# Windowed attention layers: exponentials read from PSUM, with the negated maximum as bias

## The chip, the cores and the metric

One core of a Trainium2 chip runs the whole program. The metric is the device time of one execution in microseconds: 2783.15 us, the median of three runs of the kernel before (2777.86 to 2783.55).

## The reference

The program is a chain of four blocks on a tensor of 4 sequences x 512 tokens x 128 channels. The last block, which the change touches, is six layers of windowed attention with a gated feed-forward part. One layer, for one sequence, cut to what matters:

```python
qkv = shift_tokens(x) @ Wqkv                   # 128 -> 3 x 16 heads x 64
q, k = l2norm(q) * qs, l2norm(k) * ksc         # per head
q = q * cos * scale + rotate_half(q) * sin * scale
k = k * cos / scale + rotate_half(k) * sin / scale
sim = einsum('bhwie,bhwje->bhwij', bq, bk2) * 8.0   # windows of 32, own and previous
sim = where(mask, -big, sim)
x = softmax(sim) @ v, all heads, @ Wo + x
xn = layernorm(shift_tokens(x)) * g + b
x = (a * gelu(gate)) @ W2 + b2 + x             # a, gate = xn @ W1 + b1
```

## The kernel before

The function `windowed_layers` works in 24 rounds (6 layers x 4 sequences, `ROUNDS`). A round is one sequence through one layer: four tiles of 128 tokens, and for the scores eight blocks of 64 query tokens. Each engine runs its own fixed list of steps (`ORDER`), written out by hand once per turn, and the same list is repeated turn after turn; the number of dashes behind a step says how many rounds it lags behind the turn. So three or four rounds are in flight together, and the engines are held together only by semaphores. An engine does its list strictly in order: a step that waits holds everything behind it.

The steps of one round, in the order of the data:

- SyncE `xdK` loads tile K of the input into `xs`. TensorE `PK.J` (four per tile) and `VK.J` (two per tile) are the projections, 128x512 each, into the two banks `psP`; projection u waits until the bank of projection u-2 has been read.
- ScalarE `SqK.J` squares a projection; VectorE `RK.J` sums the squares per head; VectorE `ABK.J` makes the two products of the rotation; GpSimd `ad` adds them; VectorE `Ra` makes the norms of two tiles; GpSimd `nm` multiplies by them. ScalarE `Ve` copies the values.
- TensorE `TK.J` transposes into the one bank `psT`, ScalarE `Te` copies it out to `qT` or `kT`.
- TensorE `SK.0` computes the scores of block K for all 16 heads: first the mask with a bf16 matmul (line 1544), then 32 recorded small matmuls (line 1550) into the two banks `psS[0]` and `psS[1]`, 4 groups of 96 key columns in each. VectorE `XaK.J` (twice per block) takes the maximum of each 96 columns (line 1673), waits for it, and subtracts it while moving the scores to `pb` in SBUF (line 1674). ScalarE `XeK.0` takes exp(8 x) of all 128x768 in place (line 1616). VectorE `XdK.0` sums and takes the reciprocal (lines 1680, 1681), GpSimd `XnK.0` multiplies (line 1738).
- TensorE `AtK.J` transposes the probabilities into the one bank `psA`, ScalarE `PtK.J` copies it out, TensorE `AvK.J` multiplies with the values, ScalarE `OtK.0` copies to `oT`.
- The tail of a round uses the one bank `psF`: TensorE `wo0` and `wo1` (output projection, eight recorded 128x512 matmuls each, line 1479), VectorE `xf` (line 1685) adds to `H`, SyncE `xfd` loads the shifted copy, TensorE `tr` transposes it (line 1486), VectorE `ln` normalises (lines 79, 81, 62 to 71, 85), TensorE `back` transposes back (line 1490), ScalarE `xn` scales, then three times: TensorE `gN` (gate), ScalarE `ggN` (gelu, line 1637), TensorE `aN`, VectorE `hN` (line 1695); at last TensorE `w2` (line 1504) and VectorE `out` (line 1699).
- SyncE `tl` loads the weights of the tail once per layer (`load_tail`, lines 1434 to 1439) after the last `out` of the layer before; `wo0` waits for it.

Two waits that matter below, in the kernel before: `S` waits for the subtractions of the block before (semaphore `x1`), since these free the banks `psS`; and ScalarE needs a table load each time it goes from gelu to exp or back (there are two changes each way in a turn of the list before: `Xe4`, `gg0`, `Xe5`, `Xe6`, `gg1`, `gg2`, `Xe7`).

## Time and profile before

| quantity | value |
|---|---|
| median of three runs | 2783.15 us |
| profiled execution | 2780.95 us, span 2779.2 us |
| TensorE matmul busy | 2521.7 us (91%) |
| VectorE busy | 2322.9 us (84%) |
| ScalarE busy | 1624.5 us (58%) |
| GpSimd busy | 1483.7 us (53%) |
| granted TensorE clock, mean | 0.948 |
| span of the six layers | about 995 to 2773 us |

The windowed layers take about 1778 of the 2779 us. The busy shares over the span mix stages with different limits, so the share inside this stage is what counts. On the timelines an instruction's record is longer than its place in the queue where instructions overlap: the distance from one start to the next is its pace, and the sum of paces against the length of a turn tells how much an engine waits.

### The profile page before, as it was taken

The numbers are of one execution on the slowest core, as the hardware profiler recorded it, in microseconds if no ns is written. First come the engines' busy times: TensorE is split into PE (matmuls) and PEld (weight loads), VectorE is DVE, ScalarE is ACT, GpSimd is POOL, SyncE is SP. The second block draws the span as 40 slices with busy tenths as digits, with TensorE's granted clock in tenths as the row PEclk, the third lists the DMA queues.
The fourth block names the chain that finished last, engine by engine and source line by source line (L and its number), as shares of the span: only waits on it lengthen the run. The fifth ranks groups of instructions, "written<-read, shape, count | busy, mean of one in ns | idle before, by whom it ended". The sixth has DMA issues, their size and how long they took to land. (4 is left out here: it accounts for less than half of the span.)

```text
span 2779.2 us, 60743 instructions
## 1 busy us (share of the span) xinstructions
PE 2521.7 (91%) x21942; PEld 1632.1 (59%) x21942; DVE 2322.9 (84%) x4920; ACT 1624.5 (58%) x2742; POOL 1483.7 (53%) x1226
## 2 busy tenths in 40 slices
PE   7589866999997758999999999999999999999996
PEld 4267634777774425666666666666666656666662
DVE  5878744777775678999999999999999989999982
ACT  2123224888884235666666666666666656666662
POOL 2500002767771056666666666666666656666650
PEclk9799977999997789999999999999999999999997
DMA  1000001000000021111111111111111111111110
GB/s 55 1 7 6 7 3 39 24 23 23 23 16 1 1 90 26 30 30 53 25 51 30 53 25 45 30 50 28 45 30 53 30 43 29 27 29 45 35 26 19
DMA packets 45487, 83.65 MB, mean 30 GB/s; under 512 B 13365, under 2 KB 27173, under 8 KB 44072
## 3 DMA queue, kind: packets, MB, share of 16 engines
q1 hardware_dynamic: 45224, 80.12, 10.7%
q8 instruction: 168, 2.75, 0.4%
q14 instruction: 95, 0.78, 0.1%
...
## 5 line engine op out<-in xcount | busy, mean ns | idle before, releaser
L1528 PE MATMUL w_psP<-w_qkv,w_xs 128*128 128x512 f32 x1152 | 607.3, 610 | 42.0 <-DVE w_bb L1653 28.3
L1728 POOL TENSOR_TENSOR w_ab<-w_ab,w_bb 128x512 f32<-128x512 f32 x384 | 486.0, 1274 | 173.1 <-DVE w_bb L1653 172.9
L1733 POOL TENSOR_TENSOR w_ab<-w_ab,w_nrm 128x512 f32<-128x512 f32 x384 | 395.6, 1044 | 112.4 <-DVE w_nrm L67 112.4
L1738 POOL TENSOR_TENSOR w_pb<-w_pb,w_sm 128x768 f32<-128x768 f32 x192 | 282.3, 1470 | 303.4 <-DVE w_sm L1681 303.4
L1593 ACT ACTIVATE w_sq<-w_psP 128x512 f32<-128x512 f32 x384 | 229.3, 597 | 226.3 <-PE w_psP L1528 157.9
L1012 POOL TENSOR_TENSOR e_glo<-e_hg,e_ghi 128x512 fp32r<-128x512 f32 x192 | 272.1, 1448 | 153.6 <-ACT e_ghi L991 153.6
L1652 DVE TENSOR_TENSOR w_ab<-w_psP,w_tabs 128x512 f32<-128x512 f32 x384 | 262.5, 684 | 28.1 <-ACT w_sq L1593 12.1
L1534 PEld LDWEIGHTS w_psT<-tables_all,w_ab 128*128 128x128 f32 x1536 | 179.9, 141 | 169.9 <-issue 118.0
L1621 ACT ACTIVATE w_pT<-w_psA 128x512 f32<-128x512 f32 (+1 forms) x384 | 227.5, 593 | 65.9 <-PE w_psO L1577 43.9
L1653 DVE TENSOR_TENSOR w_bb<-w_psP,w_tabs 128x512 f32<-128x512 f32 x384 | 261.4, 681 | 0.0
L1659 DVE TENSOR_REDUCE w_nrm<-w_sq 128x8 f32<-128x512 f32 x384 | 254.4, 673 | 1.1 <-ACT w_sq L1593 1.1
L1560 PEld LDWEIGHTS w_psA<-tables_all,w_pb 128*96 128x96 f32 (+1 forms) x1536 | 175.3, 134 | 135.0 <-issue 97.0
L1534 PE MATMUL w_psT<-tables_all,w_ab 128*128 128x128 f32 x1536 | 237.3, 277 | 14.9 <-POOL w_ab L1733 12.4
L1560 PE MATMUL w_psA<-tables_all,w_pb 128*96 128x128 f32 (+1 forms) x1536 | 236.2, 277 | 7.9 <-POOL w_pb L1738 6.9
L1528 PEld LDWEIGHTS w_psP<-w_qkv,w_xs 128*128 128x128 f32 x1152 | 178.7, 191 | 105.5 <-DVE w_bb L1653 54.0
L1616 ACT ACTIVATE w_pb<-w_pb 128x768 f32<-128x768 f32 x192 | 161.8, 843 | 112.2 <-DVE w_pb L1674 111.5
L1674 DVE TENSOR_TENSOR w_pb<-w_psS,w_mx 128x384 f32<-128x384 f32 x384 | 214.1, 558 | 13.2
L1673 DVE TENSOR_REDUCE w_mx<-w_psS 128x4 f32<-128x384 f32 x384 | 209.7, 546 | 9.9 <-PE w_psA L1560 7.2
L986 ACT ACTIVATE e_hh<-e_psH,e_b 128x512 f32<-128x512 f32 x256 | 172.3, 686 | 51.8 <-PE e_psH L918 51.5
L1680 DVE TENSOR_REDUCE w_sm<-w_pb 128x8 f32<-128x768 f32 x192 | 181.3, 944 | 11.9 <-ACT w_pb L1616 11.9
L1479 PE MATMUL w_psF<-w_oT,w_o 128*128 128x512 f32 x384 | 177.8, 607 | 10.5 <-DMA w_cols<-in_cols_w 9.8
L1088 DVE TENSOR_TENSOR e_hg<-e_hh,e_psR 128x512 f32<-128x512 f32 x256 | 164.2, 680 | 21.3 <-PE e_psR L931 11.6
...
## 6 DMA issues: line engine op xcount, KB each, us to landing
...
```

The costliest lines, as they stand in the source:

```text
L1012: pool.tensor_tensor(glo[b % 2][:, j, :], hg[b % 2][:, j, :], ghi[b % 2][:, j, :], ALU.subtract).then_inc(s["glo"], 1)
L1528: pe.matmul(psP[u % 2][:, :], xs[:, 128 * k:128 * (k + 1)], w_qkv[:, ds(layer % 2, 1), 512 * at:512 * at + 512], start=True, stop=True).th ...
L1534: last = pe.transpose(psT[:, 128 * q:128 * (q + 1)], ab[:, k % 2, j, 128 * q:128 * (q + 1)], c.ident[:, :])
L1560: last = pe.transpose(psA[0:rows, 128 * q:128 * (q + 1)], pb[k % 2][:, 4 * j + q, :], c.ident[:, :])
L1593: act.activation(sq[:, i % 2, :], psP[j % 2][:, :], ACT.Square).then_inc(s["sq"], 1)
L1621: act.activation(pT[0:rows, 4 * j:4 * j + 4, :], psA[0:rows, :].rearrange("p (a b) -> p a b", a=4), ACT.Copy).then_inc(s["pte"], 1)
L1652: dve.tensor_tensor(ab[:, k % 2, j, :].rearrange("p (h x d) -> p h x d", x=2, d=32), src, tab[0], ALU.mult)
L1653: dve.tensor_tensor(bb[:, i % 2, :].rearrange("p (h x d) -> p h x d", x=2, d=32), src[:, :, ::-1, :], tab[1], ALU.mult).then_inc(s["ab"], 1)
L1659: dve.tensor_reduce(nrm[k // 2][:, 0, 8 * (i % 8):8 * (i % 8) + 8], sq[:, i % 2, :].rearrange("p (h d) -> p h d", d=DH), AX_X, ALU.add).th ...
L1728: pool.tensor_tensor(a, a, bb[:, i % 2, :], ALU.add).then_inc(s["ad"], 1)
L1733: pool.tensor_tensor(a, a, nrm[k // 2][:, 1, 8 * (i % 8):8 * (i % 8) + 8].unsqueeze(2).to_broadcast([128, 8, DH]), ALU.mult).then_inc(s["n ...
L1738: pool.tensor_tensor(p, p, sm[k % 2][:, :].unsqueeze(2).to_broadcast([128, PAIRS, KEYS]), ALU.mult).then_inc(s["pn"], 1)
```

## The change

In the six windowed layers the subtraction of the maximum is no longer a step of VectorE. VectorE's step `Xm` takes the maximum with its sign turned (`negate=True`) and signals `mx`. ScalarE's step `Xe` is now run per half block (J = 0, 1) and reads the scores from PSUM: four activations of 128x96 each, one for each group of columns, with the negated maximum of that group as a per-partition bias, written to `pb`. The factor 8 of the exponent goes into the rotation tables of q. The scores' banks `psS` are now freed by ScalarE (`e`) instead of VectorE (`x1`), and the chain semaphore `max` goes. The lists of all five engines are rewritten: among other things `wo0` and `wo1` stand closer together and run two turns behind, `out` and `w2` stand at the beginning of the list, `tl` and `xfd` have moved in SyncE's list, and the three gelus stand without an exponential between them.

```diff
--- before.py
+++ after.py
@@ -144,7 +144,7 @@
     power = ((np.arange(N, dtype=np.float32) - N // 2) / 16).astype(np.float32)
     scale = (base[None, :] ** power[:, None]).astype(np.float32)
     c1, s1 = np.cos(fr).astype(np.float32), np.sin(fr).astype(np.float32)
-    for kind, f in (("q", scale), ("k", (1.0 / scale).astype(np.float32))):
+    for kind, f in (("q", 8 * scale), ("k", (1.0 / scale).astype(np.float32))):
         out["rope_cos_" + kind] = by_tile(np.concatenate([c1 * f, c1 * f], -1))
         out["rope_sin_" + kind] = by_tile(np.concatenate([-s1 * f, s1 * f], -1))
 
@@ -1328,12 +1328,12 @@
     psO = c.ps("w_psO")
     psF = c.ps("w_psF")
 
-    names = ("wa", "wf", "tab", "scl", "z", "p", "sq", "ab", "rs", "ad", "nm", "t", "te", "vx", "s", "x1", "e", "r", "pn",
+    names = ("wa", "wf", "tab", "scl", "z", "p", "sq", "ab", "rs", "ad", "nm", "t", "te", "vx", "s", "mx", "e", "r", "pn",
              "pt", "pte", "av", "ot", "f", "xf", "xsf", "yn", "xn", "gg", "hh", "out")
     s = {k: c.sem("w_s_" + k) for k in names}
     s_xs = [c.sem(f"w_s_xs{k}") for k in range(TILES)]
     s_ve = [c.sem(f"w_s_ve{j}") for j in range(2)]
-    s_norm, s_max, s_sum, s_f = (c.sem("w_s_chain_" + k) for k in ("norm", "max", "sum", "tail"))
+    s_norm, s_sum, s_f = (c.sem("w_s_chain_" + k) for k in ("norm", "sum", "tail"))
 
     def ve_done(t, r):
 
@@ -1349,33 +1349,34 @@
 
     ORDER = {
         "pe": """
-            T2.1-- wo1--- P0.2- T2.2-- P0.3- Av0.1-- T2.3-- V0.0- At2.0-- tr--- T3.0-- Av1.0-- Av1.1--
-            S4.0-- V0.1- At2.1-- P1.0- Av2.0-- T3.1-- P1.1- At3.0-- back--- P1.2- T3.2-- At3.1-- Av2.1--
-            S5.0-- P1.3- g0--- T3.3-- Av3.0-- Av3.1-- At4.0-- V1.0- a0--- V1.1- At4.1-- P2.0- S6.0--
-            Av4.0-- P2.1- T0.0- g1--- T0.1- S7.0-- Av4.1-- T0.2- P2.2- At5.0-- a1--- T0.3- At5.1-- P2.3-
-            T1.0- g2--- At6.0-- V2.0- Av5.0-- Av5.1-- S0.0- At6.1-- V2.1- a2--- P3.0- T1.1- P3.1-
-            At7.0-- T1.2- Av6.0-- S1.0- Av6.1-- P3.2- T1.3- At7.1-- P3.3- w2--- At0.0- V3.0- Av7.0--
-            S2.0- Av7.1-- V3.1- At0.1- P0.0 wo0-- T2.0- At1.0- Av0.0- S3.0- At1.1- P0.1""",
+            P1.1- g2--- At3.0-- T3.3-- P1.2- a2--- P1.3- Av2.0-- Av2.1-- S5.0-- At3.1-- V1.0- w2---
+            Av3.0-- S6.0-- Av3.1-- At4.0-- V1.1- T0.0- P2.0- At4.1-- P2.1- T0.1- At5.0-- Av4.0-- Av4.1--
+            T0.2- P2.2- At5.1-- T0.3- P2.3- Av5.0-- S7.0-- Av5.1-- V2.0- At6.0-- T1.0- V2.1- At6.1--
+            P3.0- T1.1- Av6.0-- S0.0- Av6.1-- P3.1- At7.0-- P3.2- T1.2- At7.1-- Av7.0-- S1.0- Av7.1--
+            T1.3- P3.3- wo0-- At0.0- wo1-- At0.1- T2.0- V3.0- S2.0- Av0.0- V3.1- tr-- P0.0 T2.1- P0.1
+            At1.0- T2.2- Av0.1- S3.0- T2.3- At1.1- back-- Av1.0- P0.2 T3.0- g0-- P0.3 Av1.1- S4.0- V0.0
+            At2.0- a0-- T3.1- V0.1 g1-- P1.0 T3.2- a1-- At2.1-""",
         "act": """
-            Sq1.1- xn--- Sq1.2- Xe4.0-- Te3.2-- Ot2.0-- Sq1.3- Pt3.1-- gg0--- Pt4.0-- Te3.3-- Ve1.0-
-            Ot3.0-- Ve1.1- Sq2.0- Xe5.0-- Te0.0- Pt4.1-- Xe6.0-- Te0.1- gg1--- Sq2.1- Te0.2- Pt5.0--
-            Sq2.2- Te0.3- Pt5.1-- Te1.0- Ot4.0-- Sq2.3- gg2--- Pt6.0-- Xe7.0-- Ve2.0- Ve2.1- Pt6.1--
-            Ot5.0-- Sq3.0- Te1.1- Xe0.0- Te1.2- Sq3.1- Pt7.0-- Ot6.0-- Te1.3- Sq3.2- Pt7.1-- Sq3.3-
-            Xe1.0- Pt0.0- Ot7.0-- Ve3.0- Sq0.0 Pt0.1- Xe2.0- Pt1.0- Ve3.1- Te2.0- Te2.1- Sq0.1 Xe3.0-
-            Sq0.2 Te2.2- Sq0.3 Pt1.1- Te2.3- Ot0.0- Ve0.0 Pt2.0- Te3.0- Ot1.0- Ve0.1 Sq1.0 Pt2.1- Te3.1-
-            Pt3.0-""",
+            Ot6.0-- Xe0.0- Pt7.0-- Xe0.1- Pt7.1-- Sq3.1- Te1.2- Sq3.2- Ot7.0-- Te1.3- Sq3.3- Xe1.0-
+            Pt0.0- Xe1.1- Te2.0- Ve3.0- Pt0.1- Xe2.0- Ve3.1- Te2.1- Xe2.1- Sq0.0 Te2.2- Pt1.0- Ot0.0-
+            Te2.3- Sq0.1 Pt1.1- xn-- Xe3.0- Sq0.2 Xe3.1- gg0-- Sq0.3 Te3.0- Pt2.0- Ve0.0 Te3.1- Ve0.1
+            Ot1.0- gg1-- Sq1.0 Te3.2- Pt2.1- Sq1.1 gg2-- Xe4.0- Sq1.2 Xe4.1- Pt3.0- Te3.3- Sq1.3 Ot2.0-
+            Xe5.0- Xe5.1- Pt3.1- Ve1.0 Pt4.0- Ot3.0- Ve1.1 Te0.0 Sq2.0 Pt4.1- Sq2.1 Te0.1 Xe6.0- Pt5.0-
+            Te0.2 Xe6.1- Ot4.0- Sq2.2 Te0.3 Pt5.1- Sq2.3 Xe7.0- Ve2.0 Pt6.0- Te1.0 Xe7.1- Ot5.0- Sq3.0
+            Te1.1 Pt6.1- Ve2.1""",
         "dve": """
-            Xd5.0-- AB2.0- R2.0- Xd6.0-- AB2.1- R2.1- h1--- AB2.2- Xa7.0-- Xa7.1-- AB2.3- R2.2- R2.3-
-            Xd7.0-- Xa0.0- Xa0.1- AB3.0- Xd0.0- AB3.1- h2--- R3.0- Xa1.0- AB3.2- R3.1- Xa1.1- out---
-            AB3.3- Xd1.0- R3.2- R3.3- Ra1.0- Xa2.0- Xa2.1- R0.0 AB0.0 Xd2.0- Xa3.0- Xa3.1- AB0.1 Xd3.0-
-            xf-- R0.1 AB0.2 R0.2 AB0.3 R0.3 ln-- Xa4.0- AB1.0 Xa4.1- R1.0 AB1.1 R1.1 Xd4.0- AB1.2 Xa5.0-
-            R1.2 AB1.3 R1.3 Xa5.1- Ra0.0 h0-- Xa6.0- Xa6.1-""",
+            Xm5.1-- Ra0.0- AB1.3- out--- Xd5.0-- Xm6.0-- AB2.0- AB2.1- Xm6.1-- R2.0- R2.1- Xd6.0--
+            AB2.2- Xm7.0-- AB2.3- Xm7.1-- R2.2- R2.3- Xd7.0-- R3.0- AB3.0- Xm0.0- Xm0.1- AB3.1- Xd0.0-
+            R3.1- R3.2- Xm1.0- R3.3- Ra1.0- Xm1.1- AB3.2- xf-- Xd1.0- AB3.3- Xm2.0- Xm2.1- ln-- AB0.0
+            Xm3.0- R0.0 AB0.1 Xm3.1- Xd2.0- AB0.2 R0.1 AB0.3 h0-- Xm4.0- Xd3.0- Xm4.1- R0.2 R0.3 h1--
+            R1.0 AB1.0 AB1.1 h2-- AB1.2 R1.1 Xd4.0- R1.2 Xm5.0- R1.3""",
         "pool": """
-            nm1.2- Xn7.0-- nm1.3- ad2.3- ad3.0- ad3.1- Xn0.0- ad3.2- Xn1.0- ad3.3- nm2.0- nm2.1- Xn2.0-
-            nm2.2- ad0.0 nm2.3- ad0.1 nm3.0- nm3.1- ad0.2 nm3.2- Xn3.0- ad0.3 ad1.0 nm3.3- Xn4.0- ad1.1
-            ad1.2 ad1.3 nm0.0 nm0.1 nm0.2 nm0.3 Xn5.0- ad2.0 nm1.0 Xn6.0- nm1.1 ad2.1 ad2.2""",
+            Xn4.0-- ad1.1- ad1.2- nm0.0- ad1.3- nm0.1- Xn5.0-- nm0.2- nm0.3- ad2.0- ad2.1- Xn6.0--
+            nm1.0- nm1.1- ad2.2- nm1.2- Xn7.0-- nm1.3- ad2.3- ad3.0- Xn0.0- ad3.1- nm2.0- ad3.2- nm2.1-
+            nm2.2- Xn1.0- nm2.3- ad3.3- nm3.0- nm3.1- ad0.0 nm3.2- ad0.1 nm3.3- Xn2.0- Xn3.0- ad0.2
+            ad0.3 ad1.0""",
         "sp": """
-            xfd--- xd0.0 VE2.0-- xd1.0 VE3.0-- xd2.0 VE0.0- tl-- VE1.0- xd3.0""",
+            VE3.0--- xd2.0- tl--- VE0.0-- xfd--- xd3.0- VE1.0-- xd0.0 VE2.0-- xd1.0""",
     }
 
     def unit(word):
@@ -1537,7 +1538,7 @@
                 elif kind == "S":
                     t, half = k // 2, BLK * (k % 2)
                     pe.wait_ge(s["te"], r * UR + 4 * t + 4)
-                    c.wait_apart(pe, s["x1"], r * UA + 2 * k)
+                    wait(pe, s["e"], r * UA + 2 * k)
                     for g in range(2):
                         for h in range(2):
                             rows = slice(64 * h, 64 * h + 64)
@@ -1611,9 +1612,12 @@
                                               src, ACT.Copy)
                     last.then_inc(s["te"], 1)
                 elif kind == "Xe":
-                    act.wait_ge(s["x1"], r * UA + 2 * k + 2)
-                    p = pb[k % 2][:, :, WIN * (k % 2):]
-                    act.activation(p, p, ACT.Exp, scale=8.0).then_inc(s["e"], 1)
+                    wait(act, s["pt"], r * UA + 2 * (k - 2) + 2)
+                    act.wait_ge(s["mx"], r * UA + 2 * k + j + 1)
+                    for q in range(4):
+                        last = act.activation(pb[k % 2][:, 4 * j + q, WIN * (k % 2):], psS[j][:, q * KEYS:(q + 1) * KEYS],
+                                              ACT.Exp, bias=mx[:, 4 * j + q:4 * j + q + 1])
+                    last.then_inc(s["e"], 1)
                 elif kind == "Pt":
                     rows = KEYS + WIN * (k % 2)
                     wait(act, s["av"], r * UA + 2 * (k - 1) + j + 1)
@@ -1664,18 +1668,13 @@
                     dve.wait_ge(s["rs"], r * UR + 8 * k + 8)
                     rsqrt(dve, ch, nn[:, 1, :], nn[:, 0, :], nn[:, 2, :], nn[:, 3, :], 1e-24, ALU.max, (halves, guesses))
                     ch.end()
-                elif kind == "Xa":
-                    wait(dve, s["pt"], r * UA + 2 * (k - 2) + 2)
-                    ch = Chain(dve, s_max, 1, r * UA + 2 * k + j)
-                    half = slice(4 * j, 4 * j + 4)
-                    sc = psS[j][:, 0:4 * KEYS].rearrange("p (a b) -> p a b", a=4)
+                elif kind == "Xm":
                     dve.wait_ge(s["s"], r * NBLK + k + 1)
-                    ch.link(dve.tensor_reduce(mx[:, half], sc, AX_X, ALU.max))
-                    dve.tensor_tensor(pb[k % 2][:, half, WIN * (k % 2):], sc, mx[:, half].unsqueeze(2).to_broadcast(
-                        [128, 4, KEYS]), ALU.subtract).then_inc(s["x1"], 1)
+                    dve.tensor_reduce(mx[:, 4 * j:4 * j + 4], psS[j][:, 0:4 * KEYS].rearrange("p (a b) -> p a b", a=4), AX_X,
+                                      ALU.max, negate=True).then_inc(s["mx"], 1)
                 elif kind == "Xd":
                     ch = Chain(dve, s_sum, 1, r * NBLK + k)
-                    dve.wait_ge(s["e"], r * NBLK + k + 1)
+                    dve.wait_ge(s["e"], r * UA + 2 * k + 2)
                     wait(dve, s["pn"], r * NBLK + k - 1)
                     ch.link(dve.tensor_reduce(sm[k % 2][:, :], pb[k % 2][:, :, WIN * (k % 2):], AX_X, ALU.add))
                     dve.reciprocal(sm[k % 2][:, :], sm[k % 2][:, :]).then_inc(s["r"], 1)
```

## Rows read from the trace of the kernel before

**Rows 1.** Busy us per engine, 280 us steady stretch (instructions), granted clock, DMA share.

```profile
1500.00:1780.00 280.00, 274.33 (x3010) 171.22 (x3010) 268.17 (x553) 188.19 (x315) 186.47 (x158) 1.00 0.15 39
```

**Rows 2.** Timeline (start us, us): VectorE, last step of rounds 0, 1 and 21.

```profile
1175.50 0.74 DVE L1699 SCALAR_TENSOR_TENSOR H<-w_psF,w_cols,H 128x512 f32<-128x512 f32 x1
...
1246.32 0.74 DVE L1699 SCALAR_TENSOR_TENSOR H<-w_psF,w_cols,H 128x512 f32<-128x512 f32 x1
...
2672.93 0.74 DVE L1699 SCALAR_TENSOR_TENSOR H<-w_psF,w_cols,H 128x512 f32<-128x512 f32 x1
```

**Rows 3.** Timeline of VectorE: maximum and subtraction, back to back.

```profile
1609.02 0.56 DVE L1674 TENSOR_TENSOR w_pb<-w_psS,w_mx 128x384 f32<-128x384 f32 x1
1609.50 0.55 DVE L1673 TENSOR_REDUCE w_mx<-w_psS 128x4 f32<-128x384 f32 x1
1610.08 0.56 DVE L1674 TENSOR_TENSOR w_pb<-w_psS,w_mx 128x384 f32<-128x384 f32 x1
```

**Rows 4.** Timeline of TensorE: one pair of Av, then seven in a row.

```profile
1656.23 1.15 PE L1577 MATMUL w_psO<-w_pT,tables_layer 128*64 128x64 f32 x32
...
1668.46 2.74 PE L1504 MATMUL w_psF<-w_hh,w 128*128 128x512 f32 x6
1671.03 0.60 PE L1560 MATMUL w_psA<-tables_all,w_pb 128*96 128x128 f32 x4
1671.47 1.02 PE L1528 MATMUL w_psP<-w_qkv,w_xs 128*128 128x512 f32 x2
1672.42 0.69 PE L1577 MATMUL w_psO<-w_pT,w_v 128*64 128x64 f32 x16
1673.04 0.36 PE L1544 MATMUL w_psS<-band_bf,ident_bf 64*64 64x384 bf16 x4
1673.23 0.83 PE L1550 MATMUL w_psS<-w_kT,w_qT 64*64 64x96 f32 x32
1673.99 0.68 PE L1577 MATMUL w_psO<-w_pT,w_v 128*64 128x64 f32 x16
```

**Rows 5.** Groups by line, ScalarE: busy, mean ns, idle before.

```profile
L1593 ACT ACTIVATE w_sq<-w_psP 128x512 f32<-128x512 f32 x384 | 229.3, 597 | 226.3 <-PE w_psP L1528 157.9 <-DVE w_nrm L1659 68.0 <-issue 0.2
...
L1616 ACT ACTIVATE w_pb<-w_pb 128x768 f32<-128x768 f32 x192 | 161.8, 843 | 112.2 <-DVE w_pb L1674 111.5
...
L1637 ACT ACT_TABLE_LOAD x47 | 60.3, 1283 | 0.9
...
L1637 ACT ACTIVATE w_yn<-w_psF,w_cols 128x512 f32<-128x512 f32 (+1 forms) x72 | 49.5, 687 | 11.9 <-PE w_psF L1500 11.3
...
L303 ACT ACTIVATE n_yn<-n_psX,n_shift,n_rs 128x128 f32<-128x128 f32 x32 | 11.6, 468 | 48.7 <-DVE n_shift L322 48.7
...
L1189 ACT ACTIVATE a_wv<-a_psA 128x128 f32<-128x128 f32 x1 | 0.3, 278 | 5.0 <-PE a_psA L1142 5.0
```

**Rows 6.** Timeline of ScalarE: eight 128x128 activations with two pointer operands.

```profile
22.51 2.90 ACT L303 ACTIVATE n_yn<-n_psX,n_shift,n_rs 128x128 f32<-128x128 f32 x8 [16.62 <-DVE n_shift L322]
```

**Rows 7.** Timeline of TensorE and VectorE: transposes (tr), then the normalisation, mid-stream.

```profile
1622.17 0.60 PE L1486 MATMUL w_psF<-tables_all,w_xsf 128*128 128x128 f32 x4
...
1625.26 1.20 DVE L63 SCALAR_TENSOR_TENSOR w_rs<-w_rs,w_guesses 128x4 int32<-128x4 int32 x1
...
1627.87 1.37 DVE L85 TENSOR_SCALAR w_yn<-w_psF,w_mv,w_rs 128x128 f32<-128x128 f32 x4
```

**Rows 8.** Timeline of the last microseconds: xf, tr, back.

```profile
2689.45 0.69 DVE L1685 TENSOR_TENSOR H<-w_psF,H 128x512 f32<-128x512 f32 x1
...
2693.06 0.66 PE L1486 MATMUL w_psF<-tables_all,w_xsf 128*128 128x128 f32 x4 [1.19 <-DMA w_xsf<-H]
...
2698.29 0.66 PE L1490 MATMUL w_psF<-tables_all,w_yn 128*128 128x128 f32 x4
```

**Rows 9.** Timeline of the DMA queue and TensorE at a change of layer.

```profile
2242.85 0.35 SPq L1436 DMA_DIRECT2D w_o<-in_w_o  x1
...
2250.55 6.65 PE L1479 MATMUL w_psF<-w_oT,w_o 128*128 128x512 f32 x8 [3.56 <-DMA w_cols<-in_cols_w]
```

## Prediction

> **What bounds the kernel now.** I read four views in this order. The windowed layers fill about 1778 of 2779 us, so first the last step of each round, `out`, on VectorE's timeline [rows 2]: rounds 0 and 1 end 70.82 us apart, and so do most neighbours. From round 0 to round 21 there are 21 intervals in 1497.4 us; 21 x 70.82 is 1487.2, so 10.2 us are lost elsewhere (they lie at changes of layer, below). Second, the busy table of a steady stretch [rows 1]: in 280 us VectorE is busy 268.2 (96%), TensorE 274.3 (98%), ScalarE 188.2 (67%), GpSimd 186.5 (67%). Two engines look full, so the third view must tell them apart: the paces.
>
> For TensorE I add the distances from start to start [rows 4]. A projection takes 0.86 us (0.95 when the small matmuls of Av or S follow: 1671.47 to 1672.42), a group of four transposes 0.44 (1671.03 to 1671.47), an Av step 0.62, with 0.16 less where another Av follows directly (1.15 recorded for two against 0.69 for one), the scores 0.19 + 0.76, a recorded 512-column matmul of the tail 0.43 (2.57 for six). Per turn: 24 projections 20.6, 34 groups of transposes 14.9, 16 Av 9.9 less three pairs 0.5, 8 S 7.6, 16 of `wo` 6.9, 6 of g and a 5.2, `w2` 2.6, and 0.09 for each of the 11 times that small matmuls begin, 1.0. The sum is 68.2 against a turn of 70.8: TensorE has 2.6 us per turn of waits, though its recorded busy time hides them.
>
> VectorE has none to speak of: its starts follow one another in 3-microsecond chunks of the rotation, norms and softmax, without gaps. It bounds the turn, with TensorE 2.6 us behind.
>
> **VectorE's part of the change.** The maximum has a pace of 0.58 because the subtraction waits for it, the subtraction 0.48 [rows 3]: 1.06 per half block, 16 per turn, 17.0 us. After the change a lone reduction remains. Its record is 0.55, the subtraction's 0.56 has a pace of 0.48, so I take 0.48 (0.58 if nothing overlaps): 7.7 us. The sign change rides in the same instruction; bounded by zero and 0.1 us each, it is off the bound either way. VectorE falls from about 70 to 60.5 us per turn and stops being the bound. TensorE is next, so at most 2.6 of the 9.3 us can be had.
>
> **ScalarE's part.** Removed: 8 exponentials of 768 columns, 0.843 each [rows 5], 6.7 us, and one of the two pairs of table changes, since the new list has no `Xe` between `gg0` and `gg2`: 2 x 1.28 = 2.6 us. Added: 64 activations of 96 columns with one pointer operand. No row shows this form. From below: 128 columns without pointer took 0.278, 512 took 0.597, so 0.83 ns per column and 0.251 for 96; less an overlap of 0.1 it is 0.15. From above: the two-pointer form of 128 columns takes 0.47 alone, line 303 [rows 5]. Eight of these took 2.90 us together [rows 6], that is (2.90 - 0.47) / 7 = 0.35 from start to start, an overlap of 0.12. One pointer costs 0.687 - 0.597 = 0.09 [rows 5]. So 0.251 + 0.09 - 0.12 = 0.22; I take 0.24, nearest to that row. 64 x 0.24 = 15.4. ScalarE's 67% of a turn is 47.6 us; it becomes 47.6 - 6.7 - 2.6 + 15.4 = 53.7, under 68. At 0.47 it would be 68.4.
>
> **The wait that moves.** `psS` is now free only when ScalarE has read it. From the end of S to the next S the loop is: 0.1 signal, 0.58 maximum, 0.1, eight activations 1.9, a `Pt` between the halves 0.5, 0.1: 3.3 us. The tightest place in TensorE's list is S0 to S1 (Av, P, At, P, T, At, Av: 4.4 us by rows 4). It fits by 1.1 us, at 0.24 each. Behind `S` on TensorE is everything, so if it doesn't fit, the turn pays.
>
> **The rewritten lists.** TensorE's steps are the same number, with 10 runs of small matmuls instead of 11 and two pairs of Av instead of three: 68.3 us. Three places in the lists are tight and can be priced.
>
> First, `wo1` to `tr`. The last part of the trace shows the least it takes: `xf` starts 2689.45, `tr` 2693.06 [rows 8], 3.6 plus 0.2 before it, 3.8 us. The new list puts At, T, V, S, Av, V between, 4.3 us. Cover 0.5 us; if VectorE comes late to `xf`, the excess is paid. I cost it at nothing.
>
> Second, `tr` to `back`, where the normalisation runs on VectorE. Mid-stream it takes from 1622.17 to the end of line 85 at 1629.24, 7.07 us [rows 7]; the old list put 7.5 us of work there. The new one puts P, T, P, At, T, Av, S, T, At after `tr`, 6.0 us in all. At the end of the stream, with GpSimd quiet, the same distance is 5.23 us [rows 8]. What differs is short operations that last 1.20 us instead of 0.16 mid-stream (line 63 [rows 7]). So the wait is between 0 and 1.1 us per turn. In the new lists `AB3.3` stands shortly before `ln`, so GpSimd has `ad3.3` and four `nm` to do just then; I take 1.1. A rule of the Trainium skill bears on it: "SBUF — State Buffer", section "Who interferes with whom", says that a VectorE instruction with two SBUF inputs contends with a GpSimd instruction that reads SBUF, and the later one fully blocks. The trace agrees with it in these rows; by a quiet GpSimd instead the turn would be 1.1 us shorter.
>
> Third, the change of layer. Now `tl` issues at 2242.85 and `wo0` starts at 2250.55 and still lasts 3.2 us too long [rows 9], since the loads can only begin after `out`, shortly before `wo0`. The five changes make up the 10.2 us found above. In the new list `out` stands at the beginning of the turn; what holds `tl` is then `xd2`, which needs `V2.1`, and from there to `wo0` TensorE has 11 us of steps, against about 7.7 + 3.2 us needed. Nearly all of the 10 us goes; bounds 0 and 10. I take 10.
>
> **Ramp and end.** From `wo1` to `w2` a round took 50 us of TensorE's list; now it takes 34 (list positions by the paces above), and `wo0` comes earlier. At the end less work is left after the last projection (8 us of `wo` for round 22), while the last tail, with one step waiting for the next, stays. Filling has the same chain as before. I take 7 us gained; bounds -17 and +8.
>
> **The sum.** Turn: 68.3 + 1.1 - a rounding of 0.1 for steps that overlap the wait = 69.3 us, 1.5 less than 70.8; 21 turns give 32 us. Changes of layer 10, ramp and end 7: 49 us. Against the profiled execution's own 2780.95 this is 2732 us; it lies 0.08% under the median of the runs, so no correction is made. What lies before the windowed layers isn't touched.
>
> **The rivals.**
>
> *TensorE at its floor.* The normalisation doesn't hold `back`, because GpSimd happens to be quiet or the order around it differs from my count. Turn 68.3: 21 x 2.5 = 53, with 10 and 7: 2711 us. For it: 5.23 us at the end of the stream. Against it: line 63 at 1.20 mid-stream.
>
> *Small waits take the gain.* With VectorE no longer full, TensorE meets three or four places with 0.3 us each (`back`, `tr`, P0.2 behind `AB0.0`, S4 behind `Xe3.1`, which has `Sq0.2` between its halves). Turn 70.3, half of the layer-change gain: 21 x 0.5 + 5 = 16: 2765 us. For it: the list behind `back` has P0.2 1.2 us later, and `AB0.0` needs 1.2 after `ln`; I count no slack there. Against it: each place alone is under the 0.3 us.
>
> *The activations don't overlap (slower).* If a 96-column activation costs 0.47 from start to start, the loop on `psS` is 1.4 + 8 x 0.47 = 5.2 us, 0.8 over S0 to S1, and ScalarE has 68.4 us per turn, as much as TensorE. Two full engines that exchange four buffers will not stay at 68: I take 72, so 21 x 1.2 = 25 slower, less 10 at the changes of layer: 2796 us. It decides from about 0.37 us each, where the loop fills the 4.4 us. Against it: the eight in 2.90 us. The Trainium skill ("ScalarE: Activation LUTs", section "What ACT_TABLE_LOAD costs") puts an activation with a pointer bias at about 280 ns plus 0.833 ns per column, with 93 ns of overlap; as an estimate from that page this is 0.27 us, near mine and far from the slower case.
>
> **Chances.** Forecast 0.5; TensorE at its floor 0.2; small waits 0.17; activations or another loop slower 0.1; the other 0.03 near no change. The range must reach the first three: down to 2692 (floor, with the full 17 us at ramp and end, and 10 at the layers, 2701, less the 9 by which my count of paces may be high), up to 2774 (small waits with nothing gained at the changes of layer, and some loss at the end). A measurement can tell 0.2%, 5.6 us, from no change. Faster 0.85, same 0.06, slower 0.09.
>
> **What would show it.** In the profile of the changed kernel: the distance between two `out` rows near 69.3 (68.3 and 70.3 for the rivals); VectorE's busy share of a steady stretch near 86% instead of 96%; the exponentials at 0.34 recorded and about 0.24 apart; ScalarE near 77%; one pair of table loads per turn; TensorE's largest wait `back` on `w_yn`; no wait of `wo0` on the load of the weights. I am wrong if TensorE's paces change, if `S` waits on ScalarE, or if the turns lengthen in spite of an idle VectorE.

## The result, and the profile after

The changed kernel takes 2817.31 us (median of 4 runs, 2813.17 to 2819.21), the kernel before 2782.1 (4 runs, 2777.86 to 2783.55). The ratio is 1.0124, 95% interval 1.011 to 1.0138: slower by 1.2%, where 2732 us were forecast. The profiled execution took 2818.01 us with a span of 2816.2.

I read the same views as before. First the steps `out` of rounds 0, 1 and 21 on VectorE's timeline (start us, us, engine, line, operation):

```profile
1158.33 0.74 DVE L1698 SCALAR_TENSOR_TENSOR H<-w_psF,w_cols,H 128x512 f32<-128x512 f32 x1
...
1230.57 0.74 DVE L1698 SCALAR_TENSOR_TENSOR H<-w_psF,w_cols,H 128x512 f32<-128x512 f32 x1
...
2676.72 0.74 DVE L1698 SCALAR_TENSOR_TENSOR H<-w_psF,w_cols,H 128x512 f32<-128x512 f32 x1
```

A turn is 72.24 us instead of 70.82 [rows 2]. From round 0 to round 21 it is 1518.4 us; 21 x 72.24 is 1517.0, so only 1.4 us are lost at changes of layer, where it was 10.2. At such a change the weights are now there in time. SyncE's queue and TensorE (no idle time in brackets, unlike [rows 9]):

```profile
2258.30 0.34 SPq L1437 DMA_DIRECT2D w_o<-in_w_o  x1
...
2267.57 3.60 PE L1480 MATMUL w_psF<-w_oT,w_o 128*128 128x512 f32 x8
```

Second, the busy table of the steady stretch (PE, PEld, DVE, ACT, POOL, granted clock, DMA share, GB/s), to be held against [rows 1]:

```profile
1500.00:1780.00 280.00, 271.03 (x2957) 169.89 (x2955) 234.20 (x484) 212.31 (x520) 184.40 (x155) 1.00 0.15 39
```

VectorE has fallen from 268.2 to 234.2 us (84%), ScalarE has risen from 188.2 to 212.3 (76%), and yet the turn is longer and TensorE shows less work, 271.0 instead of 274.3. VectorE and ScalarE are not full and TensorE has lost 3.3 us of work in the stretch: the time is in waits, and the last sentence of the prediction (wrong if the turns lengthen in spite of an idle VectorE) describes what happened. Third, the groups by line (busy, mean ns, idle before, what ended it):

```profile
L1618 ACT ACTIVATE w_pb<-w_psS,w_mx 128x96 f32<-128x96 f32 x1536 | 396.6, 346 | 122.9 <-DVE w_mx L1673 122.0
...
L1656 DVE TENSOR_TENSOR w_ab<-w_psP,w_tabs 128x512 f32<-128x512 f32 x384 | 262.9, 685 | 157.3 <-ACT w_sq L1594 155.4
```

VectorE now idles 157 us ahead of its rotation steps, for ScalarE's squares. The exponentials are recorded at 0.346 us; where eight stand together they take 2.09 (row at 1730.85 below), so (2.09 - 0.35) / 7 = 0.25 apart; that has a pause between the two half blocks in it, and eight without one take 1.96 (first experiment), 0.23 apart. Fourth, TensorE's waits, and what VectorE and GpSimd did at that time. Two places of a turn stand out. The first is `back` (timeline of the three engines, rows in order of time):

```profile
1701.90 1.27 POOL L1727 TENSOR_TENSOR w_ab<-w_ab,w_bb 128x512 f32<-128x512 f32 x1
...
1703.13 2.04 POOL L1732 TENSOR_TENSOR w_ab<-w_ab,w_nrm 128x512 f32<-128x512 f32 x2
1703.23 0.97 DVE L63 SCALAR_TENSOR_TENSOR w_rs<-w_rs,w_guesses 128x4 int32<-128x4 int32 x1
...
1704.23 0.97 DVE L68 TENSOR_TENSOR w_rs<-w_rs 128x4 f32<-128x4 f32 x1
...
1706.64 0.60 PE L1561 MATMUL w_psA<-tables_all,w_pb 128*128 128x128 f32 x4
...
1707.84 0.66 PE L1491 MATMUL w_psF<-tables_all,w_yn 128*128 128x128 f32 x4 [0.60 <-DVE w_yn L85]
```

The second is `V1.1`, the projection behind `At4.0`:

```profile
1730.85 2.09 ACT L1618 ACTIVATE w_pb<-w_psS,w_mx 128x96 f32<-128x96 f32 x8 [1.09 <-DVE w_mx L1673]
1731.25 2.49 POOL L1727 TENSOR_TENSOR w_ab<-w_ab,w_bb 128x512 f32<-128x512 f32 x2
...
1731.73 0.86 DVE L62 SCALAR_TENSOR_TENSOR w_nrm<-w_nrm,w_halves 128x64 f32<-128x64 f32 x1
1732.63 1.20 DVE L63 SCALAR_TENSOR_TENSOR w_nrm<-w_nrm,w_guesses 128x64 int32<-128x64 int32 x1
...
1734.85 0.64 PE L1561 MATMUL w_psA<-tables_all,w_pb 128*96 128x128 f32 x4
...
1736.29 0.68 DVE L1657 TENSOR_TENSOR w_bb<-w_psP,w_tabs 128x512 f32<-128x512 f32 x1
...
1737.02 1.13 PE L1529 MATMUL w_psP<-w_qkv,w_xs 128*128 128x512 f32 x2 [1.53 <-DVE w_bb L1657]
```

`Ra0` and `AB1.3` stand in this order in VectorE's list. The reciprocal root of `Ra0` meets two additions of GpSimd (1731.25 to 1733.74): line 62 ends at 1732.59 and line 63 at 1733.83, each within 0.1 us of the end of an addition. `AB1.3` comes behind them, frees the bank of `psP` at 1736.97, and the projection that needs it starts at 1737.02, 2.17 us after the transposes before it, which last 0.44.

With the paces of [rows 4] the distances between starts show what TensorE loses against them, from 1689.36 to 1761.60, one turn: 1.73 us at `V1.1`, 0.76 at `back`, and 1.41 in some fourteen places of 0.05 to 0.16. Together 3.90, and 72.24 - 3.90 = 68.3, the forecast's sum of paces. But the 1.41 are for the most part no waits. In half of the places a projection takes 0.96, not 0.86, though no small matmuls follow; in all of these small matmuls of `Av` come before, directly or with one group of transposes between:

```profile
1699.44 0.69 PE L1578 MATMUL w_psO<-w_pT,w_v_even 96*64 96x64 f32 x16
1700.06 1.13 PE L1529 MATMUL w_psP<-w_qkv,w_xs 128*128 128x512 f32 x2
1701.02 0.60 PE L1487 MATMUL w_psF<-tables_all,w_xsf 128*128 128x128 f32 x4
1701.46 1.02 PE L1529 MATMUL w_psP<-w_qkv,w_xs 128*128 128x512 f32 x2
```

The projection behind `Av` takes 0.96 us, the next one 0.86 (the step behind it starts at 1702.32), and both recur in the versions below that keep these lists. In a turn of the kernel before, projections behind small matmuls take 0.96 as well; the forecast counted 0.09 where small matmuls begin and nothing where they end. How much of the 1.41 is pace and how much is wait, the experiments show.

### The profile page after: what moved, and what is told of

The parts are those of the page before. It is cut to its first block and busy times, and to the rows that moved or that the text cites. A ratio compares the mean times of both kernels' runs of the same rounds, so it can differ in the third digit from the quotient of the medians.

```text
span 2816.2 us, 61678 instructions
## 1 busy us (share of the span) xinstructions
PE 2538.6 (90%) x21942; PEld 1643.9 (58%) x21942; DVE 2141.6 (76%) x4536; ACT 1794.9 (64%) x4040; POOL 1484.6 (53%) x1226
## 3 DMA queue, kind: packets, MB, share of 16 engines
q1 hardware_dynamic: 45224, 80.12, 10.5%
HBM read 31.87 MB, written 1.05 MB: 12 GB/s over the span
## 5 line engine op out<-in xcount | busy, mean ns | idle before, releaser
L1529 PE MATMUL w_psP<-w_qkv,w_xs 128*128 128x512 f32 x1152 | 616.0, 618 | 62.1 <-DVE w_bb L1657 47.1
L1618 ACT ACTIVATE w_pb<-w_psS,w_mx 128x96 f32<-128x96 f32 x1536 | 396.6, 346 | 122.9 <-DVE w_mx L1673 122.0
L1625 ACT ACTIVATE w_pT<-w_psA 128x512 f32<-128x512 f32 (+1 forms) x384 | 233.2, 607 | 53.4 <-PE w_psA L1561 51.6
```

The lines of the kernel that those rows point to most:

```text
L1529: pe.matmul(psP[u % 2][:, :], xs[:, 128 * k:128 * (k + 1)], w_qkv[:, ds(layer % 2, 1), 512 * at:512 * at + 512], start=True, stop=True).th ...
L1618: last = act.activation(pb[k % 2][:, 4 * j + q, WIN * (k % 2):], psS[j][:, q * KEYS:(q + 1) * KEYS], ACT.Exp, bias=mx[:, 4 * j + q:4 * j + ...
```

## The experiments

After the result two explanations stood against each other. One blames the operation: 64 short activations that hold `psS` until ScalarE has read it. The other blames the places in the new lists: VectorE's chains `ln` and `Ra0` run while GpSimd works, and what stands behind them comes late. "Turn" is the distance of two `out` rows in a steady stretch, with 72.24 for the changed kernel; a time without an interval is one run, beside a kernel before of 2784.24 (the first four experiments), 2783.64 (the next four) or 2783.14 (the last four).

**New steps in the old lists.** The lists of before, with the exponentials as two halves where one stood and `Xa` reduced to the maximum:

```diff
-            ... Sq1.2- Xe4.0-- Te3.2-- Ot2.0-- ...
+            ... Sq1.2- Xe4.0-- Xe4.1-- Te3.2-- Ot2.0-- ...
-            ... h1--- AB2.2- Xa7.0-- Xa7.1-- AB2.3- ...
+            ... h1--- AB2.2- Xm7.0-- Xm7.1-- AB2.3- ...
```

> The changed operations (exponentials from PSUM with the bias, VectorE without the subtraction, S waiting for ScalarE) in the lists of the kernel before, with the two halves of Xe side by side. The changed kernel repeats its turn every 72.24 us, the kernel before every 70.82. Theory L (the lists cost the time: TensorE waits 4.0 us per turn, 1.5 for V1.1 behind AB1.3, which stands behind Ra0 on VectorE, and 0.75 for back behind ln): here the turn is under 70.8, near 69.5, and the whole under 2770. Theory A (the operation costs it: ScalarE's 64 activations and its late release of the banks psS): the turn is 71.5 or more here too, and TensorE's S waits on ScalarE.

Measured: 3117.61 us (3115.53 to 3120.62), ratio 1.1203 (1.1182 to 1.1224), turn 85.2. TensorE's waits of 1500 to 1829 us, and the place of one (timeline of ScalarE and TensorE):

```profile
PE w_psS L1544 <- ACT w_pb L1617: 43.9, 19, 4.1
```

```profile
1504.33 1.28 ACT L1617 ACT_TABLE_LOAD   x1
1505.62 1.96 ACT L1617 ACTIVATE w_pb<-w_psS,w_mx 128x96 f32<-128x96 f32 x8
1507.73 0.54 PE L1544 MATMUL w_psS<-band_bf,ident_bf 64*64 64x384 bf16 x4 [4.11 <-ACT w_pb L1617]
1508.02 1.52 PE L1550 MATMUL w_psS<-w_kT,w_qT 64*64 64x96 f32 x32
```

The stretch holds 329 / 85.2 = 3.86 turns, so each loses 43.9 / 3.86 = 11.4 us because `S` waits for exponentials that stand far down in ScalarE's old list, behind a table load here. I had expected that the operation is harmless in any order, and that is wrong: `psS` was freed by VectorE, and is now freed by an engine whose list wasn't written for that. After a wait of 4.11 us the scores take 1.52 us instead of the 0.83 of [rows 4]; the granted clock of the stretch is 0.94, so part of the time is spent at TensorE's lower level, and the waits cost more than their own length. The new lists take 13 of these 14.4 us back. They are needed, and the question is what they still lose.

**One activation per half block.** This takes the number of activations away and leaves the order (it uses the maximum of the first group for all four, so part of the computation is changed):

```diff
-                    for q in range(4):
-                        last = act.activation(pb[k % 2][:, 4 * j + q, WIN * (k % 2):], psS[j][:, q * KEYS:(q + 1) * KEYS],
-                                              ACT.Exp, bias=mx[:, 4 * j + q:4 * j + q + 1])
+                    last = act.activation(pb[k % 2][:, 4 * j:4 * j + 4, WIN * (k % 2):],
+                                          psS[j][:, 0:4 * KEYS].rearrange("p (a b) -> p a b", a=4),
+                                          ACT.Exp, bias=mx[:, 4 * j:4 * j + 1])
```

> The changed kernel with one activation of 384 columns per half block instead of four of 96; all four groups get the negated maximum of the first group, so the probabilities are not the reference's. ScalarE loses 48 instructions, about 5 us per turn, and the banks psS come free 0.3 us earlier per half. Theory L: the turn stays within 0.2 of 72.24. Theory A: it falls by 1 us or more.

Measured: 2804.41 us, turn 71.79. The two waits stay, 1.28 instead of 1.53 at `V1.1` and 0.60 at `back`. So the number of activations is worth 0.45 us of a turn, between the 0.2 and the 1 that the two explanations allowed it; it is not the main cause.

**GpSimd's list, one step moved.** `ad1.2` goes behind `nm0.0`, which needs `Ra0`, so that one of the two additions beside `Ra0` is gone:

```diff
-            Xn4.0-- ad1.1- ad1.2- nm0.0- ad1.3- nm0.1- ...
+            Xn4.0-- ad1.1- nm0.0- ad1.2- ad1.3- nm0.1- ...
```

> The changed kernel with one swap in the list of GpSimd: nm0.0 ahead of ad1.2, so that ad1.2 no longer runs while Ra0 waits on VectorE. Theory L with contention between VectorE and GpSimd as the cause of the long Ra0: Ra0 ends 1.0 us sooner, V1.1 waits 0.5 instead of 1.5, the turn is 71.2. If the length of Ra0 isn't due to GpSimd, or V1.1 is held elsewhere: 72.2.

Measured: 2814.39 us, turn 72.09. VectorE and TensorE:

```profile
1514.86 0.87 DVE L62 SCALAR_TENSOR_TENSOR w_nrm<-w_nrm,w_halves 128x64 f32<-128x64 f32 x1
1515.76 0.22 DVE L63 SCALAR_TENSOR_TENSOR w_nrm<-w_nrm,w_guesses 128x64 int32<-128x64 int32 x1
...
1519.18 1.12 PE L1529 MATMUL w_psP<-w_qkv,w_xs 128*128 128x512 f32 x2 [0.56 <-DVE w_bb L1657]
1523.93 0.66 PE L1561 MATMUL w_psA<-tables_all,w_pb 128*128 128x128 f32 x4 [0.59 <-POOL w_pb L1737]
```

Line 63 falls from 1.20 to 0.22 and the wait at `V1.1` from 1.53 to 0.56, as the contention explains. But GpSimd now starts its normalisations late and is late for `At`; the gain of 1 us is given back but for 0.15. The mechanism is right, this cure isn't.

**Five GpSimd operations cut short.** `ad1.1`, `ad1.2`, `ad3.3`, `nm3.0` and `nm3.1` treat 64 of 512 columns; the rest of their work is left out. Order and waits stay.

```diff
+                    m = 64 if (k, j) in ((1, 1), (1, 2), (3, 3)) else 512
+                    pool.tensor_tensor(a[:, 0:m], a[:, 0:m], bb[:, i % 2, 0:m], ALU.add).then_inc(s["ad"], 1)
...
+                    h = 1 if (k, j) in ((3, 0), (3, 1)) else 8
```

> The changed kernel with five of GpSimd's 32 additions and products per turn cut to 64 of 512 columns (ad1.1, ad1.2, ad3.3, nm3.0, nm3.1), those that run during Ra0 and during ln; the rest of those columns is left unadded or unscaled. Theory L with contention: both waits of TensorE (1.5 and 0.75) nearly vanish, turn near 70.2. If contention isn't the cause: within 0.3 of 72.24.

Measured: 2745.65 us, turn 69.43, which is 2.81 less. Two steps of `ln` on VectorE:

```profile
1534.90 0.16 DVE L63 SCALAR_TENSOR_TENSOR w_rs<-w_rs,w_guesses 128x4 int32<-128x4 int32 x1
1535.10 0.16 DVE L68 TENSOR_TENSOR w_rs<-w_rs 128x4 f32<-128x4 f32 x1
```

Both large waits are gone, and the small ones behind `back`, with the operation and the lists of VectorE, ScalarE and TensorE untouched. That the turn now lies 0.1 from the forecast of 69.3 is chance: the forecast had a wait of 1.0 in it that is gone here, and its sum of paces was too low. What the run doesn't tell apart is blocking from less GpSimd work in all; the next experiments do, for they leave GpSimd its whole work.

**`back` one step later.**

```diff
-            ... T2.3- At1.1- back-- Av1.0- P0.2 T3.0- g0-- ...
+            ... T2.3- At1.1- Av1.0- back-- P0.2 T3.0- g0-- ...
```

> The changed kernel with back one step later in TensorE's list, behind Av1.0. Nothing is faster; 0.62 us of work is put before the step that waits 0.75. If this wait is a loss of its own, as my sum treats it, the turn falls from 72.24 to 71.6. If the turn is set by another loop through VectorE, in which TensorE's waits only add up to what is missing, it stays within 0.2 of 72.24 and another wait grows.

Measured: 2818.36 us, turn 72.26. The wait at `back` is gone and stands at P0.2:

```profile
1565.88 1.12 PE L1529 MATMUL w_psP<-w_qkv,w_xs 128*128 128x512 f32 x2 [0.54 <-DVE w_bb L1657]
```

P0.2 needs a bank that `AB0.0` frees, and `AB0.0` stands behind `ln` on VectorE. The lateness is VectorE's, so TensorE meets it wherever it next needs VectorE.

**GpSimd quiet during `ln`.** A wait is added, on work that it doesn't need: `nm3.0` starts only when the reciprocal root of `ln` is done (17 of the 20 counted steps of `ln`).

```diff
+                    if (k, j) == (3, 0):
+                        wait(pool, s_f, (r - 1) * 20 + 17)
```

> The changed kernel with one wait added on GpSimd: nm3.0 starts only when the short operations of ln are through. No work is left out. Contention: the operations of ln on lines 62 to 68 go from 3.4 us to 1.8 (two of 0.97 become 0.16), back no longer waits, the turn falls by 0.75 to 71.5. If their length has another cause: no change in them, and the turn 72.2 or longer, for GpSimd idles.

Measured: 2787.19 us, turn 71.05. GpSimd, and VectorE beside it:

```profile
1553.72 2.05 POOL L1734 TENSOR_TENSOR w_ab<-w_ab,w_nrm 128x512 f32<-128x512 f32 x2 [1.73 <-issue]
```

```profile
1551.80 0.21 DVE L62 SCALAR_TENSOR_TENSOR w_rs<-w_mv,w_halves 128x4 f32<-128x4 f32 x1
1552.04 0.16 DVE L63 SCALAR_TENSOR_TENSOR w_rs<-w_rs,w_guesses 128x4 int32<-128x4 int32 x1
1552.24 0.16 DVE L68 TENSOR_TENSOR w_rs<-w_rs 128x4 f32<-128x4 f32 x1
```

GpSimd idles 1.73 us, and the turn is 1.19 us shorter: 0.76 at `back`, the rest in small waits of the steps behind it, each 0.12 us or less (the largest in the changed kernel are ahead of the steps at 1712.34 and 1714.04). I had expected only the wait at `back`.

**GpSimd quieter during `Ra0`.** Its list goes `ad1.1 nm0.0 ad1.2 nm0.1 Xn5.0 ad1.3`, so that `Xn` of block 5 isn't pushed back.

```diff
-            Xn4.0-- ad1.1- ad1.2- nm0.0- ad1.3- nm0.1- Xn5.0-- nm0.2- nm0.3- ...
+            Xn4.0-- ad1.1- nm0.0- ad1.2- nm0.1- Xn5.0-- ad1.3- nm0.2- nm0.3- ...
```

> The changed kernel with another order of GpSimd's steps: ad1.1, nm0.0, ad1.2, nm0.1, Xn5.0, ad1.3. As in the run with nm0.0 first, ad1.2 doesn't run during Ra0; now Xn5 isn't pushed back behind ad1.3, which there cost a new wait of 0.6 us at a transposition. V1.1 waits 0.55 instead of 1.53 and no new wait: turn 71.2. If the gain is again taken back elsewhere: 72.0.

Measured: 2797.93 us, turn 71.50, between the two values expected. The wait at `V1.1` is 0.56, one of 0.18 on `nm` follows at a transposition, and that at `back` stays. `ad1.1` still lies beside line 62, and is the rest of it.

**These three together.**

```diff
+            ... T2.3- At1.1- Av1.0- back-- P0.2 T3.0- g0-- ...
+            Xn4.0-- ad1.1- nm0.0- ad1.2- nm0.1- Xn5.0-- ad1.3- nm0.2- nm0.3- ...
+                        wait(pool, s_f, (r - 1) * 20 + 17)      (ahead of nm3.0)
```

> The three edits together: back one step later, GpSimd quiet during ln and during the second half of Ra0. Nothing is left out. If the waits add up: 72.24 - 0.75 - 1.0 = 70.5 us per turn, 21 x 1.75 = 37 us less than the changed kernel, 2780, that is level with the kernel before. If all the contention near Ra0 goes as well: 70.0 and 2768. If each edit only moves the wait: above 2800.

Measured: 2769.18 us (2764.46 to 2774.16), ratio 0.9948 (0.9926 to 0.997), turn 70.28. From 72.24 the two single effects of 1.19 and 0.74 give 70.31, so they add up and moving `back` adds nothing.

**Both chains clear of GpSimd, and `Ra0` alone.** `ad1.1` and `ad1.2` go to the end of GpSimd's list, ahead of `Xn4.0`; the first of the two kernels also has the wait of `nm3.0`, the second has not.

```diff
-            Xn4.0-- ad1.1- ad1.2- nm0.0- ad1.3- nm0.1- Xn5.0-- nm0.2- nm0.3- ...
+            Xn4.0-- nm0.0- ad1.3- nm0.1- Xn5.0-- nm0.2- nm0.3- ...
-            ad0.3 ad1.0""",
+            ad0.3 ad1.0 ad1.1 ad1.2""",
```

> The changed kernel with GpSimd quiet in both places and back where it was: nm3.0 waits for the short operations of ln, and ad1.1 and ad1.2 stand before Xn4.0, in an idle time of 5 us, so that neither runs during Ra0. Ra0 goes from 3.9 us to 2.3, V1.1 no longer waits (1.53 before, 0.56 in the last version), T waits no more than 0.2: turn 69.4, the whole 21 x 0.9 = 19 us under the 2769 of the last version: 2750. If something else holds V1.1: turn 70.3, 2769.

> The changed kernel with ad1.1 and ad1.2 before Xn4.0 only; ln as in the changed kernel. Ra0 2.3 us, wait of V1.1 gone, wait of back as before 0.75: turn 72.24 - 1.6 = 70.6. Were the two waits one and the same loop, as one might think after back moved one step later changed nothing, the turn would stay above 71.5.

Measured: with both 2746.24 us (2743.51 to 2752.88), ratio to the kernel before 0.9873 (0.9857 to 0.9889), turn 69.43; with `Ra0` alone 2778.37 us, turn 70.63. The effects add up again: 1.61 for `Ra0` and 1.19 for `ln` give 69.44. It is the same turn as with the GpSimd work left out, so it was the coincidence that cost, not the amount of work. In a turn of it TensorE's record has no gap over 0.1 us. The steady stretch and the granted clock of the version with both:

```profile
1500.00:1780.00 280.00, 279.64 (x3061) 177.10 (x3060) 230.91 (x500) 220.92 (x541) 192.97 (x163) 1.00 0.15 40
```

**The same with one activation per half block** (again the maximum of the first group for all four), to see what the operation costs when the contention is gone.

> The kernel with both places quiet, and one activation of 384 columns per half block instead of four of 96 (all four groups get the negated maximum of the first group). If ScalarE's many activations still cost time now that the other waits are gone: the turn falls by over 0.3. If TensorE is at its floor (68.3 and about 1.0 for matmuls that follow small ones): within 0.2 of 69.4.

Measured: 2736.21 us, turn 69.09: 0.34 less than 69.43. The operation has a price of its own, a small one. TensorE's record has no gap left at all:

```profile
1500.00:1780.00 280.00, 280.00 (x3096) 178.10 (x3095) 232.85 (x502) 194.77 (x351) 194.33 (x164) 1.00 0.16 41
```

So about 69.1 us is what TensorE's own steps take in the new lists, not the 68.3 that the forecast added up.

**The kernel before, with GpSimd quiet during `ln`.** `ad0.3`, which lay there, gets the wait.

```diff
+                    if (k, j) == (0, 3):
+                        wait(pool, s_f, (r - 2) * 20 + 17)
```

> The kernel before (subtraction on VectorE, old lists) with one wait added on GpSimd: ad0.3 starts only when the short operations of ln are through. There ln loses two waits on GpSimd, of which this takes one (line 63, 1.20 to 0.16). VectorE is that kernel's bound, so the turn should fall by 1.0 from 70.82 to 69.8 and the whole by 22 us to 2760. If TensorE takes it back, or ad0.3 is then late for VectorE's next product: 70.5 or more, 2775.

Measured: 2762.08 us (2755.85 to 2767.04), ratio 0.9924 (0.991 to 0.9937), turn 69.79 instead of 70.82. So 21 us are to be had without the change. The best version with the change is 16 us faster than this one (2746.24 to 2762.08, both beside the same runs of the kernel before): of its gain of 1.27%, 0.76% can be had by a wait alone. More may be there: in this kernel `Ra0` hardly meets a GpSimd operation (lines 62 and 63 take 0.24 and 0.22 us on average), but `Ra1` does (0.45 and 1.19), and so does line 62 of `ln` (0.73). Freeing these wasn't tried, and neither was the old subtraction in the new lists, so what moving the subtraction is worth by itself isn't known.

## Why the prediction was wrong

**What bounds the kernel before**: two engines nearly full, VectorE ahead. The 2.6 us of waits that I read off TensorE's paces were too many: against the 69.1 us that its steps take in the new lists, the turn of 70.82 leaves 1.7. And I took VectorE for full of work, where a part of its busy time was blocking: [rows 7] showed 1.20 us for a step that takes 0.16, and it was worth 1.03 us of the turn.

**VectorE's part** held: 60.5 us per turn were forecast, and 234.2 / 280 x 72.24 = 60.4 found. **ScalarE's part** held: 0.23 to 0.25 us apart against 0.24, 212.3 / 280 x 72.24 = 54.8 us per turn against 53.7, and one pair of table loads per turn. The rival in which the activations don't overlap gave a slower kernel, but by a mechanism that isn't here; that its direction came true is chance. The loop on `psS` fits in the new lists: no `S` waits more than 0.16 us in the turn read above, and the activations' number is worth 0.34 us where nothing else is late. The first experiment shows how narrow that is: the same steps in the old lists wait 11.4 us per turn.

**The list of tight places is the step that failed.** The prediction named three, counted 1.1 us at `back`, and put the wait of `V1.1` behind `Ra0` and `AB1.3` at nothing, without a reason. It costs 1.6 us per turn. A second term, the sum of TensorE's paces, was too small: 68.3 us were counted and 69.1 are needed, since a step behind small matmuls is slower too, by 0.05 to 0.10 us. Taken from the turns of five versions, the terms are:

| term of the turn | forecast | measured | read from |
|---|---|---|---|
| TensorE's paces | 68.3 | 69.1 | turn without a wait, 69.09 |
| number of activations | 0 | 0.3 | 69.43 - 69.09 |
| `back` behind `ln`, and small waits behind it | 1.1 - 0.1 | 1.2 | 72.24 - 71.05 |
| `V1.1` behind `Ra0` and `AB1.3` | 0 | 1.6 | 72.24 - 70.63 |
| turn | 69.3 | 72.2 | |

Because of the second error the rival *TensorE at its floor*, with a turn of 68.3, was out of reach for these lists. And a turn of 69.1 is only 1.7 us under that of the kernel before: the 2.6 that the forecast started from weren't there.

I priced the blocking where the old trace showed it in the chain of `ln`, and did not look at the second function with the same chain, `Ra`. The groups of lines 62, 63 and 68 show what the new lists did (busy us, mean ns; `w_nrm` is `Ra`, `w_rs` is `ln`). Before, and then in the changed kernel:

```profile
L63 DVE SCALAR_TENSOR_TENSOR w_nrm<-w_nrm,w_guesses 128x64 int32<-128x64 int32 x48 | 33.9, 706 | 1.6
...
L62 DVE SCALAR_TENSOR_TENSOR w_nrm<-w_nrm,w_halves 128x64 f32<-128x64 f32 x48 | 16.6, 345 | 0.9
```

```profile
L62 DVE SCALAR_TENSOR_TENSOR w_nrm<-w_nrm,w_halves 128x64 f32<-128x64 f32 x48 | 35.0, 730 | 0.9
L63 DVE SCALAR_TENSOR_TENSOR w_nrm<-w_nrm,w_guesses 128x64 int32<-128x64 int32 x48 | 33.1, 691 | 1.6
L63 DVE SCALAR_TENSOR_TENSOR w_rs<-w_rs,w_guesses 128x4 int32<-128x4 int32 x24 | 22.4, 933 | 0.8
L68 DVE TENSOR_TENSOR w_rs<-w_rs 128x4 f32<-128x4 f32 x24 | 21.6, 900 | 0.8
```

In the version with both chains clear the same four rows read

```profile
L62 DVE SCALAR_TENSOR_TENSOR w_nrm<-w_nrm,w_halves 128x64 f32<-128x64 f32 x48 | 20.1, 418 | 0.9
...
L63 DVE SCALAR_TENSOR_TENSOR w_nrm<-w_nrm,w_guesses 128x64 int32<-128x64 int32 x48 | 10.8, 225 | 1.6
...
L63 DVE SCALAR_TENSOR_TENSOR w_rs<-w_rs,w_guesses 128x4 int32<-128x4 int32 x24 | 3.9, 163 | 0.8
L68 DVE TENSOR_TENSOR w_rs<-w_rs 128x4 f32<-128x4 f32 x24 | 3.9, 163 | 0.8
```

which is 112.1 - 38.7 = 73 us less VectorE time in 24 rounds, 3.1 per turn, for 2.8 us of turn. A group takes `Ra0` and `Ra1` together, and its mean hides which of them meets GpSimd. One by one, lines 62 and 63 of `Ra0` take 0.24 and 0.22 us on average in the kernel before, 0.47 and 0.22 with the new steps in the old lists, and 0.84 and 1.16 in the changed kernel; for `Ra1` it is the other way round, 0.45 and 1.19 before, 0.62 and 0.22 after. (The version with both chains clear has `Ra0` and `ln` clear; `Ra1` is as in the changed kernel, and its 0.62 makes up the mean of 418 ns.) So the blocking is not new. The rewritten lists moved most of it from `Ra1` to `Ra0`, and nearly all of that counts because in the new lists a step that frees a bank for TensorE stands directly behind each of the two chains, `AB1.3` and `AB0.0`: an engine at 84% is late there, though it waits elsewhere. The Trainium skill ("SBUF — State Buffer", section "Who interferes with whom") says that a VectorE instruction with two SBUF inputs contends with a GpSimd instruction that reads SBUF, and that the order of issue decides which of them is blocked. The timelines agree: in both chains the step that starts during a GpSimd operation ends within 0.1 us of that operation's end, and the steps of the chain that meet none take 0.16 to 0.23. I used the rule for one chain, where it held for both.

The rival of small waits named `back`, `tr`, P0.2 and S4 with 0.3 us each. Its kind was right, but it put 2.0 us on top of 68.3 where 3.9 were found, and the costliest place wasn't on its list.

**Changes of layer** held: -8.9 us (10.2 to 1.4) against -10.

**Ramp and end** were forecast at -7. The first and the last projection show them apart; of the kernel before, of the changed kernel, and of the version with both chains clear:

```profile
992.92 3.75 PE L1528 MATMUL w_psP<-w_qkv,w_xs 128*128 128x512 f32 x4 [13.57 <-DMA w_xs<-H]
...
2675.82 1.13 PE L1528 MATMUL w_psP<-w_qkv,w_xs 128*128 128x512 f32 x2
```

```profile
995.17 3.75 PE L1529 MATMUL w_psP<-w_qkv,w_xs 128*128 128x512 f32 x4 [13.13 <-DMA w_xs<-H]
...
2712.13 1.13 PE L1529 MATMUL w_psP<-w_qkv,w_xs 128*128 128x512 f32 x2
```

```profile
993.24 3.75 PE L1529 MATMUL w_psP<-w_qkv,w_xs 128*128 128x512 f32 x4 [13.30 <-DMA w_xs<-H]
...
2645.41 1.13 PE L1529 MATMUL w_psP<-w_qkv,w_xs 128*128 128x512 f32 x2
```

From first to last it is 1682.9, 1717.0 and 1652.2 us. That this stretch holds 23 turns can be seen from the last two: 64.8 us for 2.81 per turn. Against the kernel before the changed one has 34.1 = 23 x 1.42 - 8.9 + 10.3, the other -30.7 = -23 x 1.39 - 9.3 + 10.5. So filling the rotation costs 10 us more in both, where I had said that it has the same chain as before. The traces show this directly: from the first projection of round 0 to the first of round 1 it is 46.8 us before, 57.7 in the changed kernel and 57.6 in the other, so it isn't the blocking; and with the new steps in the old lists it is 48.7, so it isn't the operation either. It is the order. 4.4 us are lost up to `V1.1` of the first round:

```profile
1018.95 2.08 PE L1529 MATMUL w_psP<-w_qkv,w_xs 128*128 128x512 f32 x2 [4.48 <-DVE w_bb L1657]
```

In the new list of VectorE `AB1.3` stands behind `Ra0`, and so behind the last sum of squares that `Ra0` needs; in the old one it stands ahead of both, and in the first turn nothing else fills the time. Most of the rest is lost between 1039.91 and 1048.09, where waits of 1.52, 1.05 and 1.91 us for the first round's own steps stand ahead of the next projection; in the old lists the wait of that kind (4.62 us, until 1045.37) comes after the first projection of round 1. From 1010 to 1050 us TensorE's granted clock is 0.84 in the changed kernel and 0.93 before, with 26.6 and 27.9 us busy of 40 (0.83 in the version with both chains clear), and the projection behind the wait of 4.48 us took 2.08 us instead of 1.13, so a part of the 10 us goes to the lower level of the clock. Why it is granted stays open: with the new steps in the old lists the clock of the same stretch was 1.00, at 25.4 us busy.

From the last projection to the last `out` it is 96.4, 97.1 and 90.4: the gain of 6 or 7 us that I counted at the end comes only when the chains are clear.

**The sum of what happened**: 23 x 1.42 = 32.7 for the turns, -8.9 for the layers, 10.3 for filling, 0.8 at the end, and 2.3 ahead of the first projection, where nothing is changed: 37.2 us, where the two spans differ by 37.0. The forecast was off by 86 us: 65 in the turns (32 to be gained, 32.7 lost), 18 in ramp and end, 1 at the layers, 2.3 ahead of all.
